# First expert stage of a two-layer decoder: inner rows made transposed, value weights fetched per tile, gate weights copied by ScalarE

## The reference, cut to what matters

```python
g = jnp.einsum('th,efh->etf', xt, W1) + b1[:, None, :]
v = jnp.einsum('th,efh->etf', xt, W2) + b2[:, None, :]
h = jax.nn.silu(g) * v
eo = jnp.einsum('etf,ehf->eth', h, W3) + b3[:, None, :]
out = jnp.einsum('eth,te->th', eo, comb)
```

## Time and profile before

| what | us |
|---|---|
| median of 3 runs | 1409.94 |
| lowest and highest | 1407.51, 1413.39 |
| the profiled execution's own time | 1406.41 |
| its span in the profile | 1404.5 |
| of that PE busy (share of the span) | 1194.4 (85%) |
| DVE busy | 1038.4 (74%) |
| ACT busy | 863.6 (61%) |
| POOL busy | 555.0 (40%) |

### The profile page before, as it was taken

The page is one execution under the profiler, slowest core; times in us unless marked ns, Lnnn a source line. Parts: engine busy times, 40 slices in busy tenths (PEclk is TensorE's granted clock), DMA queues, the critical chain, the costliest instruction groups (busy, mean ns, idle before and its releaser), DMA issues. The chain is left out here.

```text
span 1404.5 us, 31524 instructions
## 1 busy us (share of the span) xinstructions
PE 1194.4 (85%) x10028; PEld 809.5 (58%) x10028; DVE 1038.4 (74%) x3150; ACT 863.6 (61%) x2465; POOL 555.0 (40%) x830
## 2 busy tenths in 40 slices
PE   3889999999999999976399958999999879983885
PEld 2456666666666666544266635555555456662885
DVE  3477888888888788875588859999999746653554
ACT  2578888878787888753166626666666634441652
POOL 1132334444352525252200066555554114553555
PEclk9899999999999999997599969999999969995997
DMA  7100000000000000000122212103000000002552
GB/s 269 41 17 14 12 15 23 24 20 28 18 30 13 29 13 22 7 22 21 54 82 82 76 53 86 39 24 96 24 21 7 2 3 9 17 20 78 161 153 84
DMA packets 71488, 63.51 MB, mean 45 GB/s; under 512 B 10510, under 2 KB 61586, under 8 KB 70688
## 3 DMA queue, kind: packets, MB, share of 16 engines
q1 hardware_dynamic: 64496, 46.85, 11.4%
q0 software_dynamic: 6400, 12.63, 2.9%
q10 hardware_dynamic: 432, 2.01, 0.4%
HBM read 43.00 MB, written 18.98 MB: 44 GB/s over the span
## 5 line engine op out<-in xcount | busy, mean ns | idle before, releaser
L701 PE MATMUL e_bank_turned<-c_matrices,e_probs 128*128 128x128 f32 x1024 | 165.1, 285 | 16.8 <-ACT e_probs_t L933 9.5
L637 POOL TENSOR_TENSOR e_rstd<-e_var_eps,c_minus_half 128x1 f32<-128x1 f32 x128 | 71.1, 576 | 249.5 <-DVE e_var_eps L969 249.2
L933 ACT ACTIVATE e_probs_t<-e_bank_turned 128x512 f32<-128x512 f32 x256 | 155.0, 606 | 16.4 <-PE e_bank_turned L701 14.8
L1055 DVE TENSOR_REDUCE e_neg_max<-e_bank_scores 128x4 f32<-128x512 f32 x160 | 109.5, 684 | 49.0 <-PE e_bank_scores L744 48.4
L701 PEld LDWEIGHTS e_bank_turned<-c_matrices,e_probs 128*128 128x128 f32 x1024 | 115.7, 144 | 40.7 <-issue 17.0
L711 PE MATMUL e_bank_mix<-e_probs_t,e_values 128*32 128x128 f32 x2048 | 112.0, 292 | 15.5 <-ACT e_probs_t L933 15.1
L892 ACT ACTIVATE e_probs<-e_scores,e_neg_max 128x128 f32<-128x128 f32 x384 | 123.3, 410 | 1.1 <-DVE e_neg_max L1091 1.1
L1665 ACT ACTIVATE d_probs_t<-d_bank_turned 128x512 f32<-128x512 f32 x128 | 77.2, 603 | 62.0 <-PE d_bank_turned L1550 61.9
L640 POOL TENSOR_TENSOR e_k_by_place<-e_q_k_k,c_matrices 128x512 f32<-128x512 f32 x64 | 66.7, 1042 | 104.9 <-DVE e_q_k_k L1099 104.9
L887 ACT ACTIVATE e_probs<-e_scores 128x512 f32<-128x512 f32 x128 | 82.1, 641 | 42.0 <-DVE e_scores L1088 41.4
L1649 ACT ACTIVATE d_probs<-d_scores 128x512 f32<-128x512 f32 x128 | 80.9, 632 | 40.0 <-DVE d_scores L1688 34.4
(11 more groups left out here) (321 smaller groups left out, 3241.6 us busy)
## 6 DMA issues: line engine op xcount, KB each, us to landing
f_up<-in_s_up SPq DMA_DIRECT2D x40, 258.0 KB
m_rows<-scratch_sorted SPq DMA_DIRECT2D x72, 64.0 KB
scratch_expert_out<-m_y SPq DMA_DIRECT2D x72, 64.0 KB
f_rows<-scratch_sorted SPq DMA_DIRECT2D x40, 65.0 KB
e_x_in<-in_x SPq DMA_DIRECT2D x32, 64.0 KB
e_ctx_in<-in_ctx SPq DMA_DIRECT2D x32, 64.0 KB
up<-in_m_wgv SPq DMA_DIRECT2D x1, 2048.0 KB
up_b<-in_m_bgv SPq DMA_DIRECT2D x1, 2048.0 KB
```

The costliest lines, as they stand in the source:

```text
L701: last = nc.tensor.transpose(turned_bank[:, j * P:(j + 1) * P], pr[k % 3][:, j, :], c["ident"][:])
L933: nc.scalar.activation(pt[k % 2][:], turned_bank[:], ACT.Copy).then_inc(probs_t_ready, 1)
L1055: nc.vector.tensor_reduce(nmax[k % 4][:], bank, AX.X, ALU.max, negate=True).then_inc(max_ready, 1)
```

## The change: what it does

The stage is written anew as `phase_gated`, in the form of `phase_last`. The inner rows come out of PE transposed, inner columns on the partitions and tokens along the free dimension: four matmuls of 128 columns with the weights as the stationary operand (two blocks of the gate matrix, two of the value matrix), and the two transpositions of the product go. The value matrix and both biases of the tile's expert come from DRAM by one transfer for each tile (128 x 260 floats, 130 KB), up to 5 tiles ahead. The gate matrices of all 8 experts are resident (1 MB), and ACT copies the one of the tile's expert to a fixed place, three buffers, two tiles ahead. ACT takes Silu with the bias in two blocks, DVE adds the value bias and multiplies in two blocks, straight from PSUM. DVE, no longer ACT, copies the transposed rows. SyncE stores the result one step later than before, behind the loads of the next step. The start of `phase_encode` fetches `m_wg` (1 MB), `m_wd` and `m_bd`; the resident value matrices and the repeated biases go.

```diff
-            load_experts(sp, keep, experts0, d, ("m_wgv", "m_wd", "m_bgv", "m_bd"))
+            sp.dma_start(experts0["gate"][:], d["m_wg"]).then_inc(keep["experts_loaded"], 16)
+            load_experts(sp, keep, experts0, d, ("", "m_wd", "", "m_bd"), (1, 3))
...
+ROWS_AHEAD0, UPS0 = 8, 5
+BLOCKS0 = FF0 // P
...
         @block.sync
         def _(sp):
-            row_of = loader(sp, "row", "tile_row", EXPERTS * REGION - P)
-            for n in range(-AHEAD, tiles):
-                k = n + AHEAD
+            row_of, expert_of = loader(sp, "row", "tile_row", EXPERTS * REGION - P), loader(sp, "in", "tile_expert", EXPERTS - 1)
+            for n in range(-ROWS_AHEAD0, tiles):
+                k = n + ROWS_AHEAD0
                 if k < tiles:
                     if k % SLOTS == 0:
                         at_rows = row_of(k // SLOTS)
...
-                if n >= 0:
-                    sp.wait_ge(y_ready, n + 1)
-                    sp.dma_start(out_rows[n * P:(n + 1) * P, :], y[n % SLOTS][:]).then_inc(y_saved[n % SLOTS], 16)
+                k = n + UPS0
+                if 0 <= k < tiles:
+                    if k % SLOTS == 0:
+                        experts = expert_of(k // SLOTS)
+                    if k >= UPS0:
+                        sp.wait_ge(hT_ready, k - UPS0 + 1)
+                    sp.dma_start(up[k % UPS0][:], dram_tile(d["m_up"], experts[k % SLOTS])).then_inc(up_loaded[k % UPS0], 16)
+                k = n - 1
+                if k >= 0:
+                    sp.wait_ge(y_ready, k + 1)
+                    sp.dma_start(out_rows[k * P:(k + 1) * P, :], y[k % SLOTS][:]).then_inc(y_saved[k % SLOTS], 16)
...
         @block.tensor
         def _(pe):
...
                     pe.wait_ge(rowsT_ready, n + 1)
+                    pe.wait_ge(up_loaded[n % UPS0], 16 * (n // UPS0 + 1))
                     if n >= SLOTS:
                         pe.wait_ge(hT_ready, n - SLOTS + 1)
-                    nc.tensor.matmul(wide[n % SLOTS][:], lhsT=rowsT[n % SLOTS][:], rhs=tile_of(e["up"], experts[n]),
-                                     start=True, stop=True).then_inc(up_done, 1)
+                    pe.wait_ge(gate_w_ready, n + 1)
+                    for k in range(2 * BLOCKS0):
+                        weights = gate_w[n % 3] if k < BLOCKS0 else up[n % UPS0]
+                        at_k = k % BLOCKS0 * P
+                        last = nc.tensor.matmul(wide[n % SLOTS][:, k * P:(k + 1) * P], lhsT=weights[:, at_k:at_k + P],
+                                                rhs=rowsT[n % SLOTS][:], start=True, stop=True)
+                    last.then_inc(up_done, 1)
...
-                if 0 <= (n := tick - LAG) < tiles:
-                    pe.wait_ge(h_ready, n + 1)
-                    for k in range(blocks):
-                        last = nc.tensor.transpose(wide[n % SLOTS][:, k * P:(k + 1) * P], h[n % SLOTS][:, k * P:(k + 1) * P],
-                                                   c["ident"][:])
-                    last.then_inc(h_transposed, 1)
-                if 0 <= (n := tick - LAG - 1) < tiles:
+                if 0 <= (n := tick - 2) < tiles:
...
         @block.vector
         def _(dve):
...
+                if 0 <= (n := tick + 2) < tiles:
+                    dve.wait_ge(rows_transposed, n + 1)
...
+                    nc.vector.tensor_copy(rowsT[n % SLOTS][:], turned_rows[n % 2][:, 0:P]).then_inc(rowsT_ready, 1)
                 if 0 <= (n := tick) < tiles:
+                    dve.wait_ge(gate_ready, n + 1)
...
+                    for k in range(BLOCKS0):
+                        block_k = slice(k * P, (k + 1) * P)
+                        last = nc.vector.scalar_tensor_tensor(
+                            out=hT[n % SLOTS][:, block_k], in0=wide[n % SLOTS][:, FF0 + k * P:FF0 + (k + 1) * P],
+                            scalar=up[n % UPS0][:, FF0 + BLOCKS0 + k:FF0 + BLOCKS0 + k + 1], in1=gateT[n % SLOTS][:, block_k],
+                            op0=ALU.add, op1=ALU.mult)
+                    last.then_inc(hT_ready, 1)
...
         @block.scalar
         def _(act):
...
+                if 0 <= (n := tick) < tiles:
+                    act.wait_ge(up_done, n + 1)
...
+                    for k in range(BLOCKS0):
+                        last = nc.scalar.activation(gateT[n % SLOTS][:, k * P:(k + 1) * P], wide[n % SLOTS][:, k * P:(k + 1) * P],
+                                                    ACT.Silu, bias=up[n % UPS0][:, FF0 + k:FF0 + k + 1])
+                    last.then_inc(gate_ready, 1)
                 if 0 <= (n := tick + 2) < tiles:
...
+                    if n >= 3:
+                        act.wait_ge(up_done, n - 2)
+                    nc.scalar.activation(gate_w[n % 3][:], tile_of(e["gate"], experts[n % SLOTS]), ACT.Copy).then_inc(gate_w_ready, 1)
```

More of the change, by code:

```diff
@@ L1200, in sem @@
         def sem(name):
-            return ctx.sem(f"{tag}_{name}")
-        wide = [ctx.enter_context(nc.psum_tensor(f"{tag}_wide{s}", [P, FF1], F32)) for s in range(SLOTS)]
-        turned_rows, sums = ([ctx.enter_context(nc.psum_tensor(f"{tag}_{name}{s}", [P, 512], F32)) for s in range(2)]
+            return ctx.sem(f"m0_{name}")
+        wide = [ctx.enter_context(nc.psum_tensor(f"m0_wide{s}", [P, FF1], F32)) for s in range(SLOTS)]
+        turned_rows, sums = ([ctx.enter_context(nc.psum_tensor(f"m0_{name}{s}", [P, 512], F32)) for s in range(2)]
@@ L1205, in phase_experts @@
                              for name in ("turned_rows", "sums"))
[L1206 to L1212, removed]
@@ L1213, in phase_experts @@
-        act_ready, h_ready, h_transposed, hT_ready = sem("act_ready"), sem("h_ready"), sem("h_transposed"), sem("hT_ready")
-        down_done, y_ready = sem("down_done"), sem("y_ready")
+        rows, rowsT, up = sb("rows", [P, P], ROWS_AHEAD0), sb("rowsT", [P, P]), sb("up", [P, FF0 + 2 * BLOCKS0], UPS0)
+        gate_w = sb("gate_w", [P, FF0], 3)
+        gateT, hT, y = sb("gateT", [P, FF0]), sb("hT", [P, FF0]), sb("y", [P, P])
+        rows_loaded, up_loaded, y_saved = ([sem(f"{name}{s}") for s in range(n)] for name, n in (
+            ("rows_loaded", ROWS_AHEAD0), ("up_loaded", UPS0), ("y_saved", SLOTS)))
@@ L1215, in phase_experts @@
+        rows_transposed, rowsT_ready, up_done, gate_ready, hT_ready, down_done, y_ready, gate_w_ready = (
+            sem(n) for n in ("rows_transposed", "rowsT_ready", "up_done", "gate_ready", "hT_ready", "down_done", "y_ready", "gate_w_ready"))
         tiles = kept["tiles"]
-        TICKS = range(-2, tiles + 4)
+        TICKS = range(-2, tiles + 3)
         block = ctx.enter_context(nc.Block())
         def loader(eng, part, table, limit):
-            sets = [[eng.alloc_register(f"{tag}_{part}{k}_{s}") for s in range(SLOTS)] for k in range(2)]
+            sets = [[eng.alloc_register(f"m0_{part}{k}_{s}") for s in range(SLOTS)] for k in range(2)]
@@ L1247, in _ @@
         def _(pe):
-            expert_of, experts = loader(pe, "up", "tile_expert", EXPERTS - 1), {}
+            expert_of = loader(pe, "down", "tile_expert", EXPERTS - 1)
             pe.wait_ge(keep["experts_loaded"], loaded)
@@ L1273, in _ @@
                         pe.wait_ge(y_ready, n - 1)
-                    for k in range(blocks):
+                    for k in range(BLOCKS0):
                         last = nc.tensor.matmul(
                             sums[n % 2][:, 0:P], lhsT=hT[n % SLOTS][:, k * P:(k + 1) * P],
-                            rhs=e["down"][:, bass.ds(experts[n], 1), k, :].rearrange("p o n -> p (o n)"),
-                            start=k == 0, stop=k == blocks - 1)
+                            rhs=e["down"][:, bass.ds(experts[n % SLOTS], 1), k, :].rearrange("p o n -> p (o n)"),
+                            start=k == 0, stop=k == BLOCKS0 - 1)
@@ L1279, in _ @@
                     last.then_inc(down_done, 1)
-                if 0 <= tick < tiles - 1 and tick % SLOTS == SLOTS - 1:
-                    experts.update(enumerate(expert_of((tick + 1) // SLOTS), tick + 1))
         @block.vector
         def _(dve):
-            expert_of, experts = loader(dve, "bias", "tile_expert", EXPERTS - 1), {}
+            expert_of = loader(dve, "bias", "tile_expert", EXPERTS - 1)
             dve.wait_ge(keep["experts_loaded"], loaded)
             for tick in TICKS:
[L1288 to L1291, removed]
-                if 0 <= (n := tick) < tiles:
[L1293 to L1301, removed]
@@ L1302, in _ @@
+                if 0 <= (n := tick + 2) < tiles:
+                    dve.wait_ge(rows_transposed, n + 1)
+                    if n >= SLOTS:
+                        dve.wait_ge(up_done, n - SLOTS + 1)
+                    nc.vector.tensor_copy(rowsT[n % SLOTS][:], turned_rows[n % 2][:, 0:P]).then_inc(rowsT_ready, 1)
+                if 0 <= (n := tick) < tiles:
+                    dve.wait_ge(gate_ready, n + 1)
                     if n >= SLOTS:
                         dve.wait_ge(down_done, n - SLOTS + 1)
```

(22 more changed lines are left out.)

36 lines of the change are left out of this document (19 added, 17 removed).

## The result

The changed kernel is slower. Its median is 1422.8 us over 5 runs (1421.18 to 1428.08) against 1409.86 for the kernel before (1407.07 to 1413.39). That is 12.9 us between the medians. The ratio is 1.0103, with a 95% interval of 1.0074 to 1.0132, some 14.5 us. The forecast was 1411.4 with a range to 1421, so the time lies above the range. SyncE's queue binds, as forecast, but by far more than I priced.

A forecast was written before the change was run, and what follows sets the result against it. PE binds before; after the change SyncE's issues bind at 1.64 us a tile against PE's 1.45. Stage 2.2 us earlier without stalls, 2.8 later with 5 of them, settled at +1.5: 1411.4 from 1409.94, range 1397 to 1421.

The forecast's parts named there:

- PE's price: PE in the changed stage: 0.89 wide step, 0.11 row transposition, 0.45 down matmuls, 1.45 us a tile, 0.19 less.
- ACT's copy: ACT's 128x256 weight copy: at most 0.42 us, with Silu 1.1 a tile, under PE's 1.45, so hidden at no cost.
- DVE's sum: DVE's work for a tile: 1.26 us, 1.4 at worst with gaps, under PE's 1.45; costed at nothing.
- the landing: Time from issue of a tile's 130 KB weight transfer until its data is there: taken as 2.3 us.
- The later start: Stage start: PE's first wide step waits for the first weights, at 692.6 instead of 691.1, 1.5 us later.
- row load to store 0.37: SyncE's queue: one of three start-to-start costs, with 0.52 twice and table reads giving 1.64 us a tile.
- the stalls: Overlong transfer issues on SyncE: 5.1 us before, hidden in spare time; each moves the end once SyncE binds; 5 taken, bounds 0 and 10.
- the check by the waits: SyncE's time not waiting, 1.05 us a tile, against the prices: these 0.03 too high, up to 2 us; settled at +1.5.
- the tail: Stage end: PE binds again for the last four tiles; last wide step near 807.6, 3.2 us to the last result, end 810.8.
- Rival C: SyncE's issues: stalls grow with transfers and traffic to 15.6 us; decides above 9 us of stalls; 1421.3 us; chance 0.14.
- Rival D: Weights late because SyncE waits for tile n-1's result before fetching for n+6; binds from 4 us landing; 1424 at 5; chance 0.03.
- Rival B: PE stays the bound, SyncE being cheaper than its rows say: -13.7 us for the tiles, 1396.4 us in all; chance 0.20.

## Why the prediction was wrong

**Right: the mechanism.** PE binds before; with a third transfer SyncE binds after; PE idles ahead of the wide step at the full clock. The third transfer alone reproduces the loss, and taking the stores away turns it into a gain. PE's price also held: 1.45 us a tile forecast, 1.45 measured once SyncE was out of the way, with the wide step at 0.89 (740.76 to 741.65), so the weights that change at every 128 columns cost what the last stage showed, not the 2.5 times that the figures of the Trainium skill (TensorE: Matmul & The Clock Gate, Back-to-back issue gap) would give. ACT's copy, DVE's sum (15.0 of 20 us busy with ACT's stores) and the landing (2.3 taken, 2.2 measured) were right or hidden. The later start was 1.5 us in the forecast, 1.4 in the profile (first wide step 4.7 us behind the first row load instead of 3.3).

**Wrong, first: the step "row load to store 0.37" beside "row load to weight load 0.53, weight load to row load 0.52".** These are pitches (start to start) of three pairs, but in the new order the third pair is store to row load, which I took at 0.52, as if the store cost 0.33 in it. Straight behind another issue the store takes 0.43, and the row load follows 0.62 after it. I had the case in hand: the store at 707.72 lasts 0.43 in the earlier trace rows, straight behind a row load, and the row that comes next in that timeline, which I left out, has the 0.62:

```profile
708.34 0.33 SPq L1238 DMA_DIRECT2D m_rows<-scratch_sorted  x1
```

The store at 704.25 came after a wait and is 0.33 long. The true sum is 0.52 + 0.38 + 0.62 = 1.52, not 1.41, plus 0.24 for table reads. Over the 65 stores ahead of the last weight load this is 7 us.

**Wrong, second: the stalls.** I took 5 us; between 700 and 812 us the pitches above their medians, less the table reads, sum to 8.8 us in the changed kernel. With them a tile takes 1.52 + 0.24 + 0.15 = 1.91 us, and 1.90 is measured from row load to row load (701.66 to 811.59, 58 tiles). From the first table read to the last weight load it is 131.8 us (685.26 to 817.09), where the forecast has 116.8 without stalls. Of these 15 us the pitches are 7; the stalls are the other 8, 3 more than taken.

**Wrong, third: the check by the waits.** It made me take off 1.3 us. It measured a queue most of whose stores waited, and these are the cheaper ones: 0.33 against 0.43. So it came out too low for a queue that never waits.

**Wrong, fourth: the tail.** From the last weight load to the end of the stage I had 6.7 us (804.1 to 810.8); it is 8.5 (817.09 to 825.6):

```profile
817.09 0.33 SPq L1245 DMA_DIRECT2D m_up<-in_m_up  x1
...
821.53 0.68 PE L1269 MATMUL m_wide<-m_rowsT,m_gate_w 128*128 128x128 f32 x4 [0.88 <-issue]
...
825.26 0.29 DVE L1317 TENSOR_TENSOR m_y<-m_sums,down_b 128x128 f32<-128x128 f32 x1 [0.90 <-PE m_sums L1284]
```

The last wide step begins 4.4 us behind its weights' issue and not 3.5, and the last result ends 4.1 behind that and not 3.2. The cause of either was not looked for.

The sum with these corrected, without the 1.3 taken off: 2.8 + 7 + 3 + 1.8 = 14.6 us, against +14.7 in the stage. **Rival C** had the place and the size but not the mechanism: the stalls do not grow with bytes, and the larger part of the miss is no stall. Its point of decision, more than 9 us, was missed by little (8.8), and that its 1421.3 lies so near the measured time is luck. **Rival D** needs SyncE to wait for results, and in the middle of the stage it doesn't: the store is always 0.38 behind the weight load, and the view of its waits names none of a weight load. The doubled bytes bring the landing to 3.5 us only, short of the 4 at which D would bind, so they alone would not rule it out. **Rival B** was right in one thing, the gain of 13.7 us for the tiles; it only needed one of the three transfers on another queue. The gain that shows in the stage is 11.7 us (125.2 to 113.5). But its reason, that PE is the busiest engine of the table, fails here: SyncE has no row in that table.

## What to carry to other kernels

A transfer added to every step is an instruction of an engine that has no row in the busy table. Before adding it, sum that engine's step from pairs in the very order of the new step and taken where the queue does not wait, and set the sum against the period that is wanted. When the queue would bind, the same edit can still pay once one of its transfers is issued by an engine with time to spare; here ACT, where the changed kernel went from 1% slower to 1% faster than the kernel before.

## What was not expected of the hardware

- A transfer issue on SyncE without address arithmetic takes 0.33 us after a wait and 0.42 to 0.44 straight behind another issue. Seen on stores and, with the fixed address, on loads.
- Long issues on SyncE (most of them 0.6 to 1.7 us) come at regular distances, and these go with PE's work more than with SyncE's own transfers or bytes. In tiles: 10.4 in the kernel before with a third transfer (703.86 to 803.76 us in five steps), 8 in the changed kernel (712.91 to 804.15 in six), 8 with doubled bytes (714.96 to 789.88 in five), 8 with ACT's stores (701.83 to 782.52 in seven), where SyncE issues two transfers for a tile instead of three, and 7.1 to 7.3 with the two added transpositions, with either queue (713.62 to 807.62 and 702.56 to 786.45, seven steps each). PE's records for a tile, matmuls and weight loads, are 18, 26, 26, 26 and 30; the products are 187, 208, 208, 208 and 213 to 219, so near each other but not equal. What links the two engines no run here shows.
- The stage ended some 6 us later with GpSimd's stores than with SyncE's or ACT's (9.1 against 2.9 us from the last result to the next phase's first transfer, one profile of each). The cause was not looked for.
